# Adapter and conditional linear layer: half of the up projection as rounded products, x turned one sample ahead

## The chip, the core and the metric

One core of a Trainium2 chip. The metric is the device time in microseconds of one execution of the whole program; the median over runs is compared.

## What is computed

32 samples, each of 512 tokens by 512 features, go through two layers with a residual around each. Each sample picks its own weights: `lang` (0 to 8) for an adapter with layer norm, `cat` (0 to 30) for a 512 x 512 linear layer. All inputs and the output are fp32.

```python
def L0(x, lang, W1, b1, W2, b2, gamma, beta):      # H = 512, A = 128
    h = relu(einsum('bsh,bha->bsa', x, W1[lang]) + b1[lang][:, None, :])
    y = x + einsum('bsa,bah->bsh', h, W2[lang]) + b2[lang][:, None, :]
    mean = y.mean(-1, keepdims=True)
    var = ((y - mean) ** 2).mean(-1, keepdims=True)
    return (y - mean) * rsqrt(var + 1e-5) * gamma[lang][:, None, :] + beta[lang][:, None, :]

x = x + L0(x, itok_B_0_8, ...)                     # x: (32, 512, 512)
out = x + (einsum('bti,bio->bto', x, W[cat]) + b[cat][:, None, :])   # cat = itok_B_0_30
```

## The kernel before

The program is written by hand, one instruction list per engine, with semaphores between them; no scheduler moves anything. A sample's tokens are four tiles of 128 (`NT`), its features four chunks of 128 (`NC`). The work is pipelined over three samples. In the step of sample s:

- PE runs, in this order: `linear_tile` 0 and 1 of sample s-2, `up` of s, `turn_norm` 0 and 1 of s-1 (transposes of the normalised activations), `linear_tile` 2 of s-2, `down` of s, `turn_norm` 2 and 3, `linear_tile` 3.
- DVE turns sample s's x into `xT` (`turn_x`, four transposes of 32x32 blocks out of `x_quad`), adds the bias to the four output tiles of s-2 (`output`), forms `x1` and `low_x1` of s-1 chunk by chunk, `low_h`, the sums `y` of s, and at the end of its step the statistics (`variance`, `inverse_deviation`: line 614 is the reciprocal, once per step).
- ScalarE (ACT) rounds the halves of W (`high_w`), normalises s-1's four tiles, does relu (`relu`), rounds `x1` (`high_x1`) and the next sample's w2 (`high_w2_of_next`, line 414), and takes the squares of `y` and the deviation.
- POOL adds the identity to W (the residual, line 348), adds b2 to x (line 358), and forms the low parts of W (line 364) and of w2 (line 338).
- SP issues nearly all transfers: per step two quarters of the next sample's `x_quad` (line 214), w2 (line 227), W (239), x by tokens (219), b2 (231), w1 (223), b (243), `params` (235) and the two output halves (249). In front of them stand three reads of ids (line 210). ScalarE issues the other two quarters of `x_quad` (line 501), right behind its second rounding of W.

Each engine takes its list strictly in order, so an instruction that waits holds up all behind it. The profile calls several tiles by another's name: w1, w2 and W all appear as `w_raw` and `w_hi`, b2 as `b_bc`; size and line tell them apart (w1 is 256 KB, line 223 on SP).

Where one step is joined to the next: `linear_tile(k, 1)` waits for the fourth output of the step before, since it writes that output's bank. SP's `store(k, 2, 1)` waits for the fourth output too, and SP's next step stands behind it. `load_params` waits for the last `low_x1`.

All buffers that are loaded ahead are double (`x_tok`, `w1_raw`, `w2_raw`, `w_raw`, `x_quad`, `xT`, ...). The loops run over two samples per pass, since the buffers alternate; samples 0 and 1 have a prologue written out by hand, in which x is turned on PE, and `keep_clock` puts matmuls of zeros into PE's pauses.

Of the kernel before, what the change touches and what calls it, by code (L numbers as in the profile page):

```python
# [3 lines left out]

class Step:

    def __init__(self, h, p):
        self.h, self.p = h, p  # L10

    def sample(self, back):

        return 2 * self.h + (self.p - back)

    def pairs(self, back):

        return self.h + (self.p - back) // 2

    def count(self, per, back, more):  # L20

        return (2 * per) * self.h + (per * (self.p - back) + more)

    def since(self, k):

        return 2 * self.h + self.p >= k if isinstance(self.h, int) else k <= 2

def adapter_then_conditional_linear(nc, x, lang_ids, cat_ids, W1, b1, W2, b2, gamma, beta, W, b, out):
# [23 lines left out]
    P = 128  # L53
    NT = T // P
    NC = H // P
    NP = 2 * NC + 1
    EPS = 1e-5
    assert A == P and NT == 4 and NC == 4 and S % 2 == 0
# [15 lines left out]
    with ctx:  # L74
# [18 lines left out]
        x_quad = [sb(f"x_quad{i}", [P, NB, NC * SQ]) for i in range(2)]  # L93
        xT = [sb(f"xT{i}", [P, NC, T]) for i in range(2)]
# [43 lines left out]
        def norm_bank(k, c):  # L138

            return n_bank[c % 2]  # L140

        def by_chunk(k):

            return k.since(2) and not (isinstance(k.h, int) and k.h == S // 2)
# [11 lines left out]
        xq_in = [sem(f"xq_in{i}") for i in range(2)]  # L156
# [42 lines left out]
        w_lo_done = sem("w_lo_done")  # L199

# [7 lines left out]
        def _(sp):  # L208
# [3 lines left out]
            def load_x_quads(s, p):  # L212
                for n in (0, 1):
                    sp.dma_start(x_quad[p][quad(n), :, :],
                                 x_quads[bass.ds(s, 1), n].rearrange("o j b f -> j (o b) f")
                                 ).then_inc(xq_in[p], 16)
# [35 lines left out]
            def step(h, p, loads=True, w_load=True, turn=True, linear=True):  # L252

                k, q = Step(h, p), 1 - p
# [19 lines left out]
                if turn:  # L274
# [3 lines left out]
                    load_b(cat_b, q)  # L278
                if linear:
# [18 lines left out]
            load_x(1, 1)  # L298
            sp.wait_ge(cat_in, 16)
            load_w(sample_id(1, 0, G), 0)  # L300
            lang1 = sample_id(0, 1, L)
            load_w1(lang1, 1)
            load_b2(lang1, 1)
# [36 lines left out]

# [535 lines left out]
```

## Time and profile before

| | us |
|---|---|
| median of 3 runs | 631.3 |
| lowest and highest | 631.16 and 632.95 |
| the profiled execution | 632.66 |
| its span, first to last instruction | 630.8 |
| granted TensorE clock, mean | 0.997 |

| engine | busy us | share of the span |
|---|---|---|
| PE | 620.4 | 98% |
| DVE | 524.0 | 83% |
| ACT | 466.2 | 74% |
| POOL | 413.6 | 66% |

A durations column can't be added up for PE: matmuls overlap, so the distance from one start to the next is what one costs. For DVE and ScalarE short overlaps of some 0.07 us between neighbours are usual. Idle time in brackets is that just before the instruction, with what ended it. "Landing" is the time from a transfer's issue until its data is there.

### The profile page before, as it was taken

The page shows a single profiled execution, that of the slowest core. Times are in us where ns is not written, and L with a number is a line of the kernel's source. Part 1 is how long each engine was busy: PE and PEld are TensorE (multiplying, and loading weights), DVE is VectorE, ACT ScalarE, POOL GpSimd, SP SyncE. Part 2 cuts the span into 40 slices and gives each one's busy share as a digit, 9 for nine tenths or more (in the row PEclk, how much of TensorE's full clock was granted, in tenths as well). Part 3 has the DMA queues.
Part 4 walks back from the last instruction along what each step waited for, and adds up shares of the span by engine and source line. Part 5 has one row for each costly group of instructions (what it writes and reads, how often), then busy time and mean ns, then how long its engine had stood idle before and what let it go on. Part 6 is the DMA issues. An engine that isn't in the chain of part 4 may idle for free.

```text
span 630.8 us, 11158 instructions
## 1 busy us (share of the span) xinstructions
PE 620.4 (98%) x2773; PEld 474.5 (75%) x2773; DVE 524.0 (83%) x1155; ACT 466.2 (74%) x709; POOL 413.6 (66%) x326
## 2 busy tenths in 40 slices
PE   8799999999999999999999999999999999999997
PEld 7567877777877777877777877777877777877786
DVE  1879888889888889888889888889888889888873
ACT  3777777787777887777787777787777787777770
POOL 3947766666766666767666866766866766866630
PEclk9899999999999999999999999999999999999999
DMA  8848899888899888899898899988899798899422
GB/s 303 265 143 247 285 295 297 262 255 276 280 294 300 258 255 275 289 287 308 259 252 274 280 291 292 274 263 259 288 286 312 253 257 274 279 289 316 167 85 100
DMA packets 125562, 166.00 MB, mean 263 GB/s; under 512 B 10834, under 2 KB 72284, under 8 KB 121456
## 3 DMA queue, kind: packets, MB, share of 16 engines
q1 hardware_dynamic: 93540, 149.59, 72.6%
q10 hardware_dynamic: 32012, 16.30, 10.7%
q8 instruction: 3, 0.05, 0.0%
q14 instruction: 7, 0.06, 0.0%
HBM read 132.17 MB, written 33.55 MB: 263 GB/s over the span
## 4 chain that ended last, share of the span: by engine, by line
PE 95%; DVE 2%; DMA 1%; issue 1%; ACT 0%; ACTq 0%; SPq 0%; DVEq 0%
PE o_bank L730 18%; PE o_bank L728 18%; PE o_bank L729 18%; PE d_bank L756 17%; PE n_bank L744 9%; PE y_bank L728 2%; PE d_bank L728 2%; PE y_bank L730 2%; PE d_bank L730 2%; PE y_bank L729 2%; PE d_bank L729 2%; DMA x_tok<-in_x 1%; DVE y L587 0%; DVE xT L693 0%; PE n_bank L806 0%
## 5 line engine op out<-in xcount | busy, mean ns | idle before, releaser
L364 POOL TENSOR_TENSOR w_lo<-w_raw,w_hi 128x512 fp32r<-128x512 f32 x128 | 163.1, 1296 | 160.1 <-ACT w_hi L439 160.1
L728 PE MATMUL o_bank<-w_hi,x1T_hi 128*128 128x512 f32 x512 | 205.6, 402 | 0.0
L730 PE MATMUL o_bank<-w_hi,x1T_lo 128*128 128x512 f32 x512 | 200.5, 392 | 0.0
L729 PE MATMUL o_bank<-w_lo,x1T_hi 128*128 128x512 f32 x512 | 199.3, 389 | 0.0
L358 POOL TENSOR_TENSOR x_tok<-x_tok,b_bc 128x512 f32<-128x512 f32 x128 | 163.8, 1303 | 38.0 <-DMA b_bc<-in_L_cond_b 38.0
L429 ACT ACTIVATE norm<-y,neg_mean_rstd,rstd 128x512 f32<-128x512 f32 x127 | 153.4, 1284 | 0.1
L465 ACT ACTIVATE squares<-y,neg_mean 128x512 f32<-128x512 f32 x128 | 91.8, 718 | 76.6 <-DVE neg_mean L593 76.6
L632 DVE SCALAR_TENSOR_TENSOR n_bank<-n_bank,params,xT 128x512 f32<-128x512 f32 x128 | 93.3, 753 | 58.8 <-PE n_bank L744 58.8
L575 DVE STREAM_TRANSPOSE xT<-x_quad 128x512 f32<-128x512 f32 x120 | 125.2, 1087 | 3.2 <-issue 3.1
L756 PE MATMUL d_bank<-xT,w_raw 128*128 128x512 f32 x256 | 115.8, 594 | 3.2 <-DVE xT L693 1.7
L730 PEld LDWEIGHTS o_bank<-w_hi,x1T_lo 128*128 128x128 f32 x512 | 96.1, 188 | 21.2
L729 PEld LDWEIGHTS o_bank<-w_lo,x1T_hi 128*128 128x128 f32 x512 | 96.4, 188 | 18.3
L728 PEld LDWEIGHTS o_bank<-w_hi,x1T_hi 128*128 128x128 f32 x512 | 96.3, 188 | 17.8
L446 ACT ACTIVATE x1T_hi<-n_bank,params 128x512 fp32r<-128x512 f32 x128 | 87.0, 689 | 27.9 <-DVE n_bank L632 26.7
L638 DVE SCALAR_TENSOR_TENSOR x1T_lo<-n_bank,params,x1T_hi 128x512 fp32r<-128x512 f32 x128 | 92.8, 747 | 6.6 <-ACT x1T_hi L446 0.2
L650 DVE TENSOR_TENSOR out_half<-o_bank,b_bc 128x512 f32<-128x512 f32 x128 | 85.9, 671 | 11.1 <-PE o_bank L730 10.9
L756 PEld LDWEIGHTS d_bank<-xT,w_raw 128*128 128x128 f32 x256 | 48.1, 190 | 53.2 <-issue 46.1
L439 ACT ACTIVATE w_hi<-w_raw 128x1024 fp32r<-128x1024 f32 x64 | 67.6, 1056 | 12.9 <-DVE out_half L650 12.7
L744 PEld LDWEIGHTS n_bank<-ident,norm 128*128 128x128 f32 x512 | 60.3, 145 | 20.7 <-issue 15.6
L744 PE MATMUL n_bank<-ident,norm 128*128 128x128 f32 x512 | 66.8, 273 | 0.4 <-ACT norm L429 0.4
L348 POOL TENSOR_TENSOR w_raw<-w_raw,ident 128x512 f32<-128x512 f32 x32 | 50.5, 1577 | 0.0
L587 DVE SCALAR_TENSOR_TENSOR y<-d_bank,x_tok 128x512 f32<-128x512 f32 x64 | 43.7, 683 | 1.9 <-PE d_bank L730 1.9
(59 smaller groups left out, 524.9 us busy)
## 6 DMA issues: line engine op xcount, KB each, us to landing
w_raw<-in_L_cond_W SPq DMA_DIRECT2D x32, 1024.0 KB, 6.6
out<-out_half SPq DMA_DIRECT2D x63, 512.0 KB, 3.9
x_tok<-in_x SPq DMA_DIRECT2D x31, 1024.0 KB, 8.9
w_raw<-in_L_cond_W SPq DMA_DIRECT2D x64, 256.0 KB, 6.4
b_bc<-in_L_cond_b SPq DMA_DIRECT2D x64, 256.0 KB, 9.5
x_quad<-in_x SPq DMA_DIRECT2D x60, 256.0 KB, 3.9
x_quad<-in_x ACTq DMA_DIRECT2D x60, 256.0 KB, 3.9
x_tok<-in_x ACTq DMA_DIRECT2D x1, 512.0 KB, 3.3
```

The lines of the kernel that those rows point to most:

```text
L358: pool.tensor_tensor(x_tok[p][:, t, :], x_tok[p][:, t, :], b2_bc[p][:, :], ALU.add).then_inc(x_b2_done, 1)
L364: pool.tensor_tensor(w_lo[q][:, c, :], w_raw[q][:, c, :], w_hi[q][:, c, :].bitcast(F32), ALU.subtract).then_inc(w_lo_done, 1)
L429: act.activation(dst, src, ACT.Identity, scale=rstd[:, t:t + 1], bias=neg_mean_rstd[:, t:t + 1]).then_inc(norm_done, 1)
L465: act.activation(squares[:, t, :], y[:, t, :], ACT.Square, bias=neg_mean[:, t:t + 1], accum_out=sq_sum[:, t:t + 1]).then_inc(sq_done, 1)
L575: dve.transpose(xT[p][:, c, :].rearrange("p (b j) -> p b j", j=SQ), x_quad[p][:, :, c::NC]).then_inc(xT_done, 1)
L632: dve.scalar_tensor_tensor(norm_bank(k, c)[:, :], norm_bank(k, c)[:, :], params[q][:, c:c + 1], xT[q][:, c, :], ALU.mult, ALU.add).then_in ...
L638: dve.scalar_tensor_tensor(x1T_lo[q][:, c, :], norm_bank(k, c)[:, :], params[q][:, NC + c:NC + c + 1], x1T_hi[q][:, c, :].bitcast(F32), AL ...
L728: pe.matmul(acc, lhs_hi, rhs_hi, start=first, stop=False)
L729: pe.matmul(acc, lhs_hi, rhs_lo, start=False, stop=False)
L730: return pe.matmul(acc, lhs_lo, rhs_hi, start=False, stop=last)
L744: ins = pe.transpose(norm_bank(k, c)[:, t * P:(t + 1) * P], norm[:, t, c * P:(c + 1) * P] if by_chunk(k) else norm[:, t, c::NC], ident[:, :])
L756: ins = pe.matmul(d_bank[0][:, :], w1_raw[k.p][:, c, :], xT[k.p][:, c, :], start=c == 0, stop=c == NC - 1)
```

## The change

1. Of `up`'s four chunks, 0 and 1 (`NS = 2`) become products of rounded parts; chunks 2 and 3 stay plain fp32 and go first. The parts are made one sample ahead: ScalarE rounds chunks 0 and 1 of the next sample's w1 (128x256) and of its turned x (128x1024), POOL subtracts to get the low parts.
2. So the next sample's x must be turned a step earlier: DVE's `turn_next_x` in step s turns sample s+1. `xT` has three tiles in place of two, `x_quad` one in place of two. Its reload waits until the four turns of the step are done; it stands behind b in SP's list and behind relu in ScalarE's.
3. The buffers now alternate by two and by three, so all loops take six samples per pass (`ROUND = 6`); steps 2 to 7 are written out and, on all engines but PE, the last six too; four passes are left for the loop on PE and three on the others.
4. POOL's order: the low parts of W are made in two pairs with b2's additions between; behind w2's low part come w1's and x's.
5. The prologue is rebuilt: x's first turns by token tile and not by chunk, `w1` and `b2` of sample 1 loaded ahead of the first W, x of sample 1 turned half before and half after `down` of 0, quarters of sample 2 loaded and turned there, four normalisations all on ScalarE, 8 and 12 zero matmuls in place of 4 and 6.

In SP's list, one regular step; the rows begin behind the three reads of ids. `w_raw ... 128x512` is w2 at line 227 (245 after) and w1 at line 223 (241 after), `128x2048` is W. Before:

```order
L214 ISA [waits xT_done]
L214 DMA x_quad<-in_x 32x16x128
L214 ISA
L214 DMA x_quad<-in_x 32x16x128
L227 ISA [waits y_done]
L227 DMA w_raw<-in_L_cond_W 128x512
L239 ISA [waits w_lo_done]
L239 DMA w_raw<-in_L_cond_W 128x2048
L219 DMA x_tok<-in_x 128x4x512
L231 ISA
L231 DMA b_bc<-in_L_cond_b 128x512
L223 DMA w_raw<-in_L_cond_W 128x512
```

After, SP's list at the same place:

```order
L245 ISA [waits y_done]
L245 DMA w_raw<-in_L_cond_W 128x512
L257 ISA [waits w_lo_done]
L257 DMA w_raw<-in_L_cond_W 128x2048
L237 DMA x_tok<-in_x 128x4x512
L249 ISA
L249 DMA b_bc<-in_L_cond_b 128x512
L241 DMA w_raw<-in_L_cond_W 128x512
L261 ISA [waits out_done]
L261 DMA b_bc<-in_L_cond_b 128x512
L232 DMA x_quad<-in_x 32x16x128 [waits xT_done]
L232 DMA x_quad<-in_x 32x16x128
```

The two quarters of `x_quad` moved from the head to behind b; the other loads keep their order, w1 as the fourth behind w2.

ScalarE's list in a regular step, from behind its second rounding of W. `w_hi ... 128x512` is the rounding of the next w2. Before:

```order
L501 DMA x_quad<-in_x 32x16x128 [waits xT_done]
L501 DMA x_quad<-in_x 32x16x128
L456 ACTIVATE d_bank<-d_bank,params 128x512 [waits params_in0,up_done]
L459 ACTIVATE hT_hi<-d_bank 128x512 [waits relu_done]
L446 ACTIVATE x1T_hi<-n_bank,params 128x512 [waits x1_done,params_in1]
L446 ACTIVATE x1T_hi<-n_bank,params 128x512 [waits x1_done]
L414 ACTIVATE w_hi<-w_raw 128x512 [waits down_done,w2_in1]
L465 ACTIVATE squares,sq_sum<-y,neg_mean 128x512 [waits mean_done,y_done] x3
L446 ACTIVATE x1T_hi<-n_bank,params 128x512 [waits x1_done] x2
```

After, ScalarE's list at the same place; `w_hi ... 128x256` is the rounding of the next w1's two chunks:

```order
L501 ACTIVATE d_bank<-d_bank,params 128x512 [waits params_in1,up_done]
L504 ACTIVATE hT_hi<-d_bank 128x512 [waits relu_done]
L558 DMA x_quad<-in_x 32x16x128 [waits xT_done]
L558 DMA x_quad<-in_x 32x16x128
L491 ACTIVATE x1T_hi<-n_bank,params 128x512 [waits x1_done,params_in0]
L491 ACTIVATE x1T_hi<-n_bank,params 128x512 [waits x1_done]
L459 ACTIVATE w_hi<-w_raw 128x512 [waits down_done,w2_in0]
L521 ACTIVATE w_hi<-w_raw 128x256 [waits w1_in0]
L526 ACTIVATE xs_hi<-xT 128x1024 [waits xT_done]
L510 ACTIVATE squares,sq_sum<-y,neg_mean 128x512 [waits mean_done,y_done] x3
L491 ACTIVATE x1T_hi<-n_bank,params 128x512 [waits x1_done] x2
```

The two transfers moved behind relu, and two roundings with a wait for w1 and one for xT stand in front of the first square.

The diff, cut to its core:

```diff
     def __init__(self, h, p):
         self.h, self.p = h, p
+        self.b, self.x = p % 2, p % 3
...
-        x_quad = [sb(f"x_quad{i}", [P, NB, NC * SQ]) for i in range(2)]
-        xT = [sb(f"xT{i}", [P, NC, T]) for i in range(2)]
+        x_quad = sb("x_quad", [P, NB, NC * SQ])
+        xT = [sb(f"xT{i}", [P, NC, T]) for i in range(3)]
+
+        xs_hi = sb("xs_hi", [P, NS, T], F32R)
+        xs_lo = sb("xs_lo", [P, NS, T], F32R)
+        w1_hi = sb("w1_hi", [P, NS, A], F32R)
+        w1_lo = sb("w1_lo", [P, NS, A], F32R)
...
                     cat_b = sample_id(1, k.sample(1), G)
                 if loads:
-                    sp.wait_ge(xT_done, k.count(NC, 0, 0))
-                    load_x_quads(k.sample(-1), q)
...
+                    sp.wait_ge(xT_done, k.count(NC, 0, 2 * NC))
+                    load_x_quads(k.sample(-2))
                 if linear:
                     store(k, 2, 0)
...
             step(0, 1, linear=False)
-            with sp.Fori(1, S // 2 - 1) as h:
-                step(h, 0)
-                step(h, 1)
-            step(S // 2 - 1, 0)
-            step(S // 2 - 1, 1, loads=False)
-            step(S // 2, 0, loads=False, w_load=False)
-
-            last = Step(S // 2, 1)
+            for p in range(2, 2 + ROUND):
+                step(0, p)
+            with sp.Fori(1, S // ROUND - 1) as h:
+                for p in range(2, 2 + ROUND):
+                    step(h, p)
+            for p in range(2, 2 + ROUND):
+                s = S - ROUND + p - 2
+                step(S // ROUND - 1, p, quads=s + 2 < S, loads=s + 1 < S)
+            step(S // ROUND, 2, quads=False, loads=False, w_load=False)
...
+            def low_w1(k):
+
+                pool.wait_ge(w1_hi_done, k.count(1, 0, 0))
+                pool.tensor_tensor(w1_lo[:, :, :], w1_raw[1 - k.b][:, 0:NS, :], w1_hi[:, :, :].bitcast(F32),
+                                   ALU.subtract).then_inc(w1_lo_done, 1)
+
+            def low_xs(k):
+
+                pool.wait_ge(xs_hi_done, k.count(1, 0, 0))
+                for c in range(NS):
+                    pool.tensor_tensor(xs_lo[:, c, :], xT[(k.x + 1) % 3][:, c, :], xs_hi[:, c, :].bitcast(F32),
+                                       ALU.subtract).then_inc(xs_lo_done, 1)
...
-                        for c in range(NC):
-                            low_w(c)
+                        low_w(0)
+                        low_w(1)
                     if adapter:
                         plus_b2(2)
                         plus_b2(3)
+                    if turn:
+                        low_w(2)
+                        low_w(3)
                 if follow:
                     low_w2(q, k.count(1, -1, 1))
+                    if k.since(1):
+                        low_w1(k)
+                        low_xs(k)
...
+            def high_w1_of_next(k):
+
+                act.wait_ge(w1_in[1 - k.b], 16 * k.pairs(-1) + 16)
+                act.activation(w1_hi[:, :, :], w1_raw[1 - k.b][:, 0:NS, :], ACT.Copy).then_inc(w1_hi_done, 1)
+
+            def high_xs_of_next(k):
+
+                act.wait_ge(xT_done, k.count(NC, 0, NC + NS))
+                act.activation(xs_hi[:, :, :], xT[(k.x + 1) % 3][:, 0:NS, :], ACT.Copy).then_inc(xs_hi_done, 1)
 
...
                     normalise(k, t)
                 high_w(k, 2)
-                if follow:
-                    load_next_x_quads(k)
                 if adapter:
                     relu(k)
+                if follow and not k.last(S - 2):
+                    load_next_x_quads(k)
...
                 high_x1(k, 1)
                 if follow:
                     high_w2_of_next(k)
+                    high_w1_of_next(k)
+                    high_xs_of_next(k)
                 if adapter:
...
-                load_x_quads(k.sample(-1), 1 - k.p)
+                act.wait_ge(xT_done, k.count(NC, 0, 2 * NC))
+                load_x_quads(k.sample(-2))
 
...
-                act.activation(xT[0][:, c, :], first_xT_bank(c)[:, :], ACT.Copy).then_inc(xT_done, 1)
+                copy_first_xT(0, c)
             high_w2(0, 0)
             relu(k0)
+            load_x_quads(2)
+            copy_first_xT(1, 0)
+            copy_first_xT(1, 1)
+            high_w(k1, 0)
+            high_w2_of_next(k0)
             for t in range(NT):
                 square(k0, t)
             deviation(k0)
-            high_w(k1, 0)
-            high_w2_of_next(k0)
-
-            normalise(k1, 0)
-            normalise(k1, 1)
-            normalise(k1, 2)
-            load_next_x_quads(k1)
             relu(k1)
+            for t in range(NT):
+                normalise(k1, t)
             high_w(k1, 2)
+            square(k1, 0)
+            square(k1, 1)
             high_x1(k1, 0)
             high_x1(k1, 1)
-            high_w2_of_next(k1)
-            square(k1, 0)
-            square(k1, 1)
+            square(k1, 2)
+            square(k1, 3)
             high_x1(k1, 2)
             high_x1(k1, 3)
-            square(k1, 2)
-            square(k1, 3)
             deviation(k1)
-
-            with act.Fori(1, S // 2 - 1) as h:
-                step(h, 0)
-                step(h, 1)
-            step(S // 2 - 1, 0)
-            step(S // 2 - 1, 1, follow=False)
-            step(S // 2, 0, adapter=False, follow=False)
+            high_w2_of_next(k1)
+            load_next_x_quads(k1)
+            high_w1_of_next(k1)
+            high_xs_of_next(k1)
+
+            for p in range(2, 2 + ROUND):
+                step(0, p)
+            with act.Fori(1, S // ROUND - 1) as h:
+                for p in range(2, 2 + ROUND):
+                    step(h, p)
+            for p in range(2, 2 + ROUND):
+                step(S // ROUND - 1, p, follow=S - ROUND + p - 1 < S)
+            step(S // ROUND, 2, adapter=False, follow=False)
...
 
-            def turn_x(k, c):
-
-                p = k.p % 2
+            def turn_next_x(k, c):
+
                 if c == 0:
-                    dve.wait_ge(xq_in[p], 16 * NQ * k.pairs(0))
-                dve.transpose(xT[p][:, c, :].rearrange("p (b j) -> p b j", j=SQ),
-                              x_quad[p][:, :, c::NC]).then_inc(xT_done, 1)
+                    dve.wait_ge(xq_in, k.count(16 * NQ, 0, 0))
+                dve.transpose(xT[(k.x + 1) % 3][:, c, :].rearrange("p (b j) -> p b j", j=SQ),
+                              x_quad[:, :, c::NC]).then_inc(xT_done, 1)
 
...
-                                  ALU.mult, ALU.add).then_inc(norm_done, 1)
+            low_h(k1)
+            turn_next_x(k1, 0)
+            y_pair(k1, 0)
+            y_pair(k1, 1)
             x1(k1, 0)
             x1(k1, 1)
-            low_h(k1)
             low_x1(k1, 0)
             low_x1(k1, 1)
-            y_pair(k1, 0)
             x1(k1, 2)
             x1(k1, 3)
             low_x1(k1, 2)
             low_x1(k1, 3)
-            y_pair(k1, 1)
+            turn_next_x(k1, 1)
             variance(k1)
             inverse_deviation(k1)
-
-            with dve.Fori(1, S // 2) as h:
-                step(h, 0)
-                step(h, 1)
-            step(S // 2, 0, adapter=False)
+            turn_next_x(k1, 2)
+            turn_next_x(k1, 3)
+
+            for p in range(2, 2 + ROUND):
+                step(0, p)
+            with dve.Fori(1, S // ROUND - 1) as h:
+                for p in range(2, 2 + ROUND):
...
             def up(k):
 
-                pe.wait_ge(w1_in[k.p], 16 * k.pairs(0) + 16)
+                acc, parts = d_bank[0][:, :], NS if k.since(2) else 0
+                pe.wait_ge(w1_in[k.b], 16 * k.pairs(0) + 16)
                 if k.since(1):
                     pe.wait_ge(y_done, k.count(NT, 0, 0))
-                for c in range(NC):
+                for c in range(parts, NC):
                     pe.wait_ge(xT_done, k.count(NC, 0, c + 1))
-                    ins = pe.matmul(d_bank[0][:, :], w1_raw[k.p][:, c, :], xT[k.p][:, c, :],
-                                    start=c == 0, stop=c == NC - 1)
+                    ins = pe.matmul(acc, w1_raw[k.b][:, c, :], xT[k.x][:, c, :], start=c == parts, stop=c == NC - 1 and not parts)
+                if parts:
+                    pe.wait_ge(w1_lo_done, k.count(1, 2, 1))
+                for c in range(parts):
+                    pe.wait_ge(xs_lo_done, k.count(NS, 2, c + 1))
+                    ins = split_product(acc, w1_hi[:, c, :], w1_lo[:, c, :], xs_hi[:, c, :], xs_lo[:, c, :],
+                                        False, c == parts - 1)
                 ins.then_inc(up_done, 1)
 
...
-                step(h, 1)
-
-
-            k = Step(S // 2, 0)
+            for c in range(NC):
+                turn_norm(k1, c)
+            keep_clock(12, o_bank[1])
+
+            for p in range(2, 2 + ROUND):
+                step(0, p)
+            with pe.Fori(1, S // ROUND) as h:
+                for p in range(2, 2 + ROUND):
+                    step(h, p)
+
+
+            k = Step(S // ROUND, 2)
             linear_tile(k, 0)
             linear_tile(k, 1)
```

## Rows read from the trace of the kernel before

**Rows 1.** The page's busy shares, and its chain by engine:

```profile
PE 620.4 (98%) x2773; PEld 474.5 (75%) x2773; DVE 524.0 (83%) x1155; ACT 466.2 (74%) x709; POOL 413.6 (66%) x326
...
PE 95%; DVE 2%; DMA 1%; issue 1%; ACT 0%; ACTq 0%; SPq 0%; DVEq 0%
```

**Rows 2.** The timeline of PE around `up` (start, us, instructions):

```profile
306.34 0.40 PE L730 MATMUL o_bank<-w_hi,x1T_lo 128*128 128x512 f32 x1
306.57 3.60 PE L756 MATMUL d_bank<-xT,w_raw 128*128 128x512 f32 x8
310.01 1.04 PE L744 MATMUL n_bank<-ident,norm 128*128 128x128 f32 x8
```

**Rows 3.** The timeline of DVE, each step's reciprocal:

```profile
302.49 0.17 DVE L614 RECIPROCAL r<-std 128x4 f32<-128x4 f32 x1
...
321.52 0.17 DVE L614 RECIPROCAL r<-std 128x4 f32<-128x4 f32 x1
...
340.30 0.17 DVE L614 RECIPROCAL r<-std 128x4 f32<-128x4 f32 x1
```

**Rows 4.** ScalarE's x_quad loads in the prologue: duration, start, landing:

```profile
L501 ACTq DMA_DIRECT2D x_quad<-in_x x2: 339/886/1432, 22.2 to 22.5; - x2
...
DMA to landing us min/median/max: 9.4/10.1/10.7
```

**Rows 5.** The timeline of ScalarE in a regular step:

```profile
308.38 1.06 ACT L439 ACTIVATE w_hi<-w_raw 128x1024 fp32r<-128x1024 f32 x1
...
313.59 0.62 ACT L414 ACTIVATE w_hi<-w_raw 128x512 fp32r<-128x512 f32 x1
316.46 0.73 ACT L465 ACTIVATE squares<-y,neg_mean 128x512 f32<-128x512 f32 x1 [2.24 <-DVE neg_mean L593]
```

**Rows 6.** The timeline of SP's loads in the same step:

```profile
306.36 0.89 SPq L214 DMA_DIRECT2D x_quad<-in_x  x2
307.43 0.36 SPq L227 DMA_DIRECT2D w_raw<-in_L_cond_W  x1
...
309.05 0.36 SPq L231 DMA_DIRECT2D b_bc<-in_L_cond_b  x1
309.51 0.47 SPq L223 DMA_DIRECT2D w_raw<-in_L_cond_W  x1
```

**Rows 7.** SP's line 223 (w1) in that step, issue to landing:

```profile
DMA to landing us min/median/max: 9.8/9.8/9.8
```

**Rows 8.** The timeline of POOL in that step:

```profile
315.77 1.58 POOL L348 TENSOR_TENSOR w_raw<-w_raw,ident 128x512 f32<-128x512 f32 x1
318.81 2.56 POOL L358 TENSOR_TENSOR x_tok<-x_tok,b_bc 128x512 f32<-128x512 f32 x2 [1.45 <-DMA b_bc<-in_L_cond_b]
```

**Rows 9.** SP's line 231 (b2) in that step, issue to landing:

```profile
DMA to landing us min/median/max: 9.6/9.6/9.6
```

**Rows 10.** The timeline of SP in the prologue, w2 and w1:

```profile
18.72 0.37 SPq L227 DMA_DIRECT2D w_raw<-in_L_cond_W  x1
...
20.77 0.59 SPq L223 DMA_DIRECT2D w_raw<-in_L_cond_W  x1
```

**Rows 11.** SP's line 223 (w1) in the prologue, issue to landing:

```profile
DMA to landing us min/median/max: 11.1/11.1/11.1
```

**Rows 12.** The page's DMA queue of ScalarE: packets, MB, share:

```profile
q10 hardware_dynamic: 32012, 16.30, 10.7%
```

**Rows 13.** The timeline of DVE, the fourth output of a step:

```profile
320.80 0.68 DVE L650 TENSOR_TENSOR out_half<-o_bank,b_bc 128x512 f32<-128x512 f32 x1
```

**Rows 14.** The timeline of DVE, two of a step's four turns:

```profile
322.40 2.07 DVE L575 STREAM_TRANSPOSE xT<-x_quad 128x512 f32<-128x512 f32 x2
```

**Rows 15.** The page's DMA issues, ScalarE's x_quad loads:

```profile
x_quad<-in_x ACTq DMA_DIRECT2D x60, 256.0 KB, 3.9
```

**Rows 16.** The timeline of PE in the prologue, behind a pause:

```profile
27.36 0.50 PE L728 MATMUL d_bank<-w_hi,hT_hi 128*128 128x512 f32 x1 [1.69 <-DVE hT_lo L580]
```

**Rows 17.** Busy times, clock (PEclk) and DMA by stretch, 28 to 29 us:

```profile
28.00:29.00 1.00, 1.00 (x4) 0.81 (x3) 0.97 (x2) 0.17 (x1) 1.00 (x1) 0.50 1.08 350
```

More of the change, by code:

```diff
@@ L10, in __init__, with last @@
         self.h, self.p = h, p
+        self.b, self.x = p % 2, p % 3
     def sample(self, back):
-        return 2 * self.h + (self.p - back)
+        return ROUND * self.h + (self.p - back)
     def pairs(self, back):
-        return self.h + (self.p - back) // 2
+        return ROUND // 2 * self.h + (self.p - back) // 2
     def count(self, per, back, more):
-        return (2 * per) * self.h + (per * (self.p - back) + more)
+        return (ROUND * per) * self.h + (per * (self.p - back) + more)
     def since(self, k):
-        return 2 * self.h + self.p >= k if isinstance(self.h, int) else k <= 2
+        return ROUND * self.h + self.p >= k if isinstance(self.h, int) else k <= 2
+    def last(self, s):
+        return isinstance(self.h, int) and ROUND * self.h + self.p == s
 def adapter_then_conditional_linear(nc, x, lang_ids, cat_ids, W1, b1, W2, b2, gamma, beta, W, b, out):
@@ L56, in adapter_then_conditional_linear @@
     NP = 2 * NC + 1
+    NS = 2
     EPS = 1e-5
[L58 removed]
+    assert A == P and NT == 4 and NC == 4 and S % ROUND == 2 and S > 2 * ROUND
     NQ, SQ = 4, 32
@@ L138, in norm_bank @@
         def norm_bank(k, c):
-            return n_bank[c % 2]
+            return y_bank[c - 2] if c >= 2 and not k.since(2) else n_bank[c % 2]
         def by_chunk(k):
-            return k.since(2) and not (isinstance(k.h, int) and k.h == S // 2)
+            return k.since(2) and not k.last(S)
         def down_bank(t):
@@ L155, in adapter_then_conditional_linear @@
         first_b1_in = sem("first_b1_in")
-        xq_in = [sem(f"xq_in{i}") for i in range(2)]
+        xq_in = sem("xq_in")
         x_in = [sem(f"x_in{i}") for i in range(2)]
@@ L250, in store, with step @@
                              ).then_inc(stored[half], 16)
-            def step(h, p, loads=True, w_load=True, turn=True, linear=True):
-                k, q = Step(h, p), 1 - p
+            def step(h, p, quads=True, loads=True, w_load=True, turn=True, linear=True):
+                k = Step(h, p)
+                p, q = k.b, 1 - k.b
                 if loads:
@@ L586, in y_tile @@
                 dve.wait_ge(x_b2_done, k.count(NT, 0, t + 1))
-                dve.scalar_tensor_tensor(y[:, t, :], down_bank(t)[:, :], 1.0, x_tok[k.p][:, t, :],
+                if k.since(1) and not k.since(2):
+                    dve.wait_ge(norm_done, t + 1)
+                dve.scalar_tensor_tensor(y[:, t, :], down_bank(t)[:, :], 1.0, x_tok[k.b][:, t, :],
                                          ALU.mult, ALU.add, accum_out=y_sum[:, t:t + 1]
@@ L596, in y_pair @@
             def y_pair(k, i):
-                if i == 0 and k.since(1):
+                if i == 0 and k.since(2):
                     dve.wait_ge(norm_done, k.count(NT, 0, 0))
@@ L690, in _ @@
             y_pair(k0, 1)
-            for c in range(NC):
+            dve.wait_ge(xT_done, NC + 2)
+            for c in (2, 3):
                 dve.wait_ge(first_xT_turned, NC + c + 1)
@@ L710, in _ @@
             low_x1(k1, 3)
-            y_pair(k1, 1)
+            turn_next_x(k1, 1)
             variance(k1)
             inverse_deviation(k1)
-            with dve.Fori(1, S // 2) as h:
-                step(h, 0)
-                step(h, 1)
-            step(S // 2, 0, adapter=False)
+            turn_next_x(k1, 2)
[3 more added lines that the diff above has]
+            with dve.Fori(1, S // ROUND - 1) as h:
+                for p in range(2, 2 + ROUND):
+                    step(h, p)
+            for p in range(2, 2 + ROUND):
+                step(S // ROUND - 1, p, follow=S - ROUND + p - 1 < S)
+            step(S // ROUND, 2, adapter=False, follow=False)
             for t in range(NT):
-                output(Step(S // 2, 1), t)
+                output(Step(S // ROUND, 3), t)
         @block.tensor
@@ L811, in _ @@
             pe.wait_ge(ident_done, 3)
-            for c in range(NC):
-                turn_first_x(k0, c)
+            turn_first_x()
             up(k0)
```

142 lines of the change are left out of this document (76 added, 66 removed).

## Prediction

> **What bounds the kernel now.** I read the page's busy shares and its chain first: PE is busy 98% of the span and holds 95% of the chain that ended last [rows 1]. Then one regular step of PE in order of time [rows 2]: each rounded matmul starts 0.23 us after the one before, the eight pieces of `up` stand from 306.57 to 310.01, and nothing waits. The third view is the distance from one step's reciprocal to the next [rows 3]: 340.30 - 302.49 = 37.81 us for two steps, 18.9 us for one; the two differ by 0.26 us (19.03 and 18.78), once per pass of the loop of two. So PE's own work is the bound, and a shorter `up` is worth its full length if no other cycle is longer than the new step. The profiled execution took 632.66 us, of which the span is 630.8; the median of the runs is 631.3, 1.4 us less. I add to 632.66 and take off 1.4 at the end.
>
> **The change, part by part.**
>
> *Two chunks of `up`.* A plain fp32 chunk is two pieces: 3.44 / 4 = 0.86 us. A product of rounded parts is three matmuls of 0.23 us, 0.68 us [rows 2]. Two chunks save 2 x 0.18 = 0.36 us in each of 30 steps, 10.7 us, all on PE's path.
>
> *The loop of six.* Of 15 loop passes 4 stay. If the 0.26 us belongs to the loop head, that gives back up to 11 x 0.26 = 2.9 us; at worst nothing.
>
> *x turned one sample ahead.* DVE's four transposes stay four per step, at the same place; what they read was loaded a whole step earlier, from one quarter tile. SP and ScalarE reload it once the step's turns are through, about 7.5 us into the step, and it is needed some 15 us later. Where such loads ran against a full queue they took 9.4 to 10.7 us [rows 4], so this costs nothing in a regular step.
>
> *ScalarE gets two more operations*, between the rounding of w2 and the first square. From 128x512 in 0.62 us and 128x1024 in 1.06 us [rows 5], rounding w1's 128x256 is about 0.40 us and x's 128x1024 1.0 us of issue distance: 1.4 us. Their cover is the 2.24 us that the first square waits for DVE [rows 5]; 0.8 us of that is left. Alone, this is free.
>
> *POOL gets three more subtractions*, 0.7 + 2 x 1.3 = 3.3 us per step, in front of the identity's addition. It is busy 66% of the span [rows 1], so some 6 us a step are idle, and the reordering fills an idle stretch in front of w_lo. From the end of ScalarE's rounding of w2, 314.2, it takes a handoff of some 0.3 us, w2's 1.3, the 3.3 and the addition's 1.58 [rows 8]: 320.7, ahead of ScalarE's next rounding of W, which comes behind the fourth output, at about 321.5. Free, barely.
>
> *The new wait, which decides.* The rounding of w1 waits until w1 **of the next sample** has landed, and this load is not moved: it stands fifth in SP's list of the same step. Until now nobody needed it before the next `up`, 15 us later. In the trace it is issued at 309.51 [rows 6] and lands 9.8 us later [rows 7], at 319.3. ScalarE reaches the place of the new operation at 313.59 + 0.62 = 314.2 [rows 5], and with 0.8 us of cover would have to have the data by 315.0. Neighbouring evidence that landings are real: POOL waits 1.45 us until 318.81 for b2 [rows 8], the transfer just ahead of w1 in that queue, issued at 309.05 and landed 9.6 us after [rows 6, 9].
>
> The change takes SP's x_quad loads from in front of these transfers (SP starts 1.07 us earlier, 306.36 for 307.43 [rows 6]). But ScalarE's two x_quad loads go from behind the normalisation's dispatch to behind relu, into the middle of these transfers. So I must ask how long w2, W, x, b2 and w1 take from an empty queue with ScalarE's loads arriving some us later. The trace holds exactly that case once, in the prologue: w2 is issued at 18.72, w1 at 20.77 [rows 10], w1 lands 11.1 us after [rows 11], at 31.9, and ScalarE's quarters start at 22.2 beside it [rows 4]. That is 13.15 us from the first issue. The regular step, with SP's quarters ahead instead, gives nearly the same: 319.3 - 306.36 = 12.95 us. In the new kernel ScalarE's quarters start about 4.5 us after w2 and not 3.4, so I estimate that 0.25 us less of them comes in front: **12.9 us**.
>
> From the other side: a step's ScalarE quarters are worth 10.7% of the span [rows 12] over 30 steps, 2.25 us. If none of them delayed w1, it would take 13.15 - 2.25 = 10.9 us.
>
> Who waits behind it: squares 0 to 2, x1T_hi 2 and 3, square 3 and the deviation are queued behind that operation on ScalarE. x1T_lo 2 and 3 on DVE wait for x1T_hi, the fourth output (ends 320.80 + 0.68 = 321.48 [rows 13], 0.04 us before the reciprocal at 321.52, and so at 302.45 in the step before [rows 3]) is queued behind them, SP's second store waits for that output, and SP's next loads stand behind the store. That closes a cycle, step to step:
> - fourth output ended, to SP's first load: 306.36 - 302.45 = 3.9 us [rows 3, 6]; in the steps of the other half of the loop some 3.5; I take 3.7 us
> - first load issued to w1 landed: 12.9 us
> - landing to ScalarE's start, as POOL's after b2: 318.81 - (309.05 + 9.6), 0.15 us
> - rounding w1 and x: 0.40 + 1.0 us
> - first square's start to the end of the fourth output: 321.48 - 316.46 = 5.0 us, which was back to back on ScalarE up to x1T_hi and on DVE from there [rows 5, 13].
>
> Sum: 3.7 + 12.9 + 0.15 + 1.4 + 5.0 = **23.15 us a step**, 4.25 us over 18.9. PE's 18.6 us no longer matter; PE will stand idle about 4.6 us a step before its second tile, since that tile's bank waits for the fourth output.
>
> Steps 3 to 30 do this, 28 of them: 28 x 4.25 = 119 us. In step 2 SP has one thing more in front: the quarters for sample 3 wait for the four turns at the prologue's end, the last two of them (2.07 us [rows 14]) after the statistics. 2.07 + 0.9 (two issues) + 0.5 (params) + 3.0 (three id reads) instead of the 0.4 us of before gives some 6.1 us, then 12.9 + 6.55: a step of about 26 to 27 us for 18.2 before, 9 us more. The rest of the rebuilt prologue is copies and turns in another order; PE's waits there are under 2 us each and I give it -1 us, with 3 us to either side. Steps 31 and on have no rounding ahead: 0.
>
> Total: 632.66 + 119 + 9 - 1 = 759.7; on the median's footing **758 us**.
>
> **What the skill adds.** Rows show ScalarE's quarters, alone in a regular step, landing after 3.9 us at the median [rows 15] and beside a full SP queue after 9.4 to 10.7 [rows 4]: they share. The Trainium skill (DMA: Bandwidth & Descriptors, Queues, rings and completion order) says that each DMA engine takes packets in turn from the queues that have work. By that rule the small packets are nearly all through before w1 is, and the sum stays; if SP's queue instead went first, it would be the 10.9 us. The trace agrees with the rule, by the same landings.
>
> **The rivals.**
> - *The wait, but w1 lands sooner* (10.9 us): a step of 21.15 us, 2.25 x 28 = 63 us less, 695 us. For it: nobody has measured the new order, and PE's pause may push relu and the quarters later. Against it: the prologue's 13.15.
> - *No wait that counts; faster*. The mechanism: the five transfers, 2.9 MB, land by 315.0, 8.6 us after SP's first issue. Then PE stays the bound: 632.66 - 10.7 - 2.9 - 1 - 1.4 = 617 us. It decides at 8.6 us; the shortest row is 12.95. Also a misreading of which sample's w1 is waited for would end here.
> - *A small wait*: 9 to 10.5 us and a step of 19.3 to 20.8; 640 to 690 us.
> - *The clock falls too, slower still*. After PE stood 1.69 us [rows 16], the granted clock was 0.50, the 1.2 GHz level, in the next whole microsecond [rows 17]. With 4.6 us idle per step I expect such a stretch in every step. From the fourth output on PE has four tiles of twelve matmuls, one `up` and two groups of turns ahead, 4 x 2.74 + 3.08 + 1.6 = 15.6 us, due by 22.5, so up to 6.7 us of its work at half speed are hidden. If 10 us of it ran at half speed, the step would be 0.2 + 25.6 + 0.7 = 26.5 us and the time 28 x 3.35 = 94 us longer, near 850 us.
>
> **How the numbers follow.** The forecast (730 to 790 us, with the cycle's terms at 3.5 to 3.9, 12.0 to 13.7 and the prologue's 3 us): 0.72. Sooner landing (690 to 730): 0.13. Small wait (640 to 690): 0.05. PE-bound and faster: 0.04. Same: 0.01. Clock or another wait on top, over 790 us: 0.05. The range takes the first two, 690 to 790 us, about 0.85. Within 0.3% is what a measurement here can't tell from no change. Faster 0.04, same 0.01, slower 0.95.
>
> **What the profile would show.** Right: ScalarE's waits led by `w_hi` or `squares` on the w1 load, some 4 us in each of about 29 steps, beginning with the 128x256 operation; PE idle 4 to 5 us before `o_bank`'s second tile; reciprocals 23 us apart; w1 landing 11 us after its issue; PE's eight pieces of `up` gone to four plus six rounded ones, about 3.1 us; chain shared by ScalarE, DVE, SP and DMA. Wrong: reciprocals 18.6 apart with PE at 98% (the load landed in time); PE waiting for POOL's xs_lo (POOL the bound); or a granted clock of 0.5 through most of a step.

## The result: 11% slower, each step waits for w1

| | before | after |
|---|---|---|
| median, same chip | 632.05 us | 701.48 us |
| lowest and highest | 631.16 to 632.95 | 699.54 to 702.79 |
| span of the profiled execution | 630.8 us | 700.9 us |
| granted TensorE clock, mean | 0.997 | 0.97 |

The ratio is 1.1103 (1.1084 to 1.1123; such brackets are 95% intervals). The kernel before takes about 631.2 or 632.9 us from one execution to the next (granted clock 1.0 or 0.997), and with a fourth run beside the first three its median is 632.05. The page of the kernel after, its busy shares and its chain by engine, against [rows 1]:

```profile
PE 635.4 (91%) x2853; PEld 496.4 (71%) x2853; DVE 522.2 (75%) x1152; ACT 498.3 (71%) x772; POOL 509.0 (73%) x416
...
DMA 32%; SPq 16%; ACT 15%; PE 13%; DVE 10%; issue 10%; POOL 2%; ACTq 1%; DVEq 0%; POOLq 0%
```

PE held 95% of the chain before and holds 13% now; a third of it is a transfer. Who waited for whom in the kernel after (total, times, longest):

```profile
ACT w_hi L521 <- DMA w_raw<-in_L_cond_W: 109.7, 28, 6.5
POOL w_lo L368 <- ACT w_hi L521: 89.2, 29, 5.6
DVE x1T_lo L704 <- ACT x1T_hi L491: 82.1, 30, 5.4
...
PE o_bank L798 <- DVE x1T_lo L704: 50.9, 24, 4.0
```

L521 is the rounding of w1, and its releaser (what ended the wait) is the load. The three rows under it are the same lateness passed on, from ScalarE to POOL, to DVE and to PE.

One step of the kernel after: first SP's loads of w2 (L245) and w1 (L241), then the time from w1's issue to its landing in that step, then ScalarE's timeline against [rows 5]:

```profile
327.19 0.38 SPq L245 DMA_DIRECT2D w_raw<-in_L_cond_W  x1
...
329.25 0.80 SPq L241 DMA_DIRECT2D w_raw<-in_L_cond_W  x1
```

```profile
DMA to landing us min/median/max: 11.0/11.0/11.0
```

```profile
333.90 0.62 ACT L459 ACTIVATE w_hi<-w_raw 128x512 fp32r<-128x512 f32 x1
340.24 0.42 ACT L521 ACTIVATE w_hi<-w_raw 128x256 fp32r<-128x256 f32 x1 [5.72 <-DMA w_raw<-in_L_cond_W]
340.56 1.04 ACT L526 ACTIVATE xs_hi<-xT 128x1024 fp32r<-128x1024 f32 x1
341.51 0.70 ACT L510 ACTIVATE squares<-y,neg_mean 128x512 f32<-128x512 f32 x1
...
343.63 1.24 ACT L491 ACTIVATE x1T_hi<-n_bank,params 128x512 fp32r<-128x512 f32 x2
```

w1 is issued at 329.25 and ScalarE starts at 340.24, the moment it lands. The squares now stand back to back behind it; the first had waited for DVE in [rows 5]. DVE at the end of the same step, and the reciprocal that opened it, against [rows 3, 13]:

```profile
323.78 0.17 DVE L680 RECIPROCAL r<-std 128x4 f32<-128x4 f32 x1
...
344.33 1.41 DVE L704 SCALAR_TENSOR_TENSOR x1T_lo<-n_bank,params,x1T_hi 128x512 fp32r<-128x512 f32 x2 [4.70 <-ACT x1T_hi L491]
345.65 0.68 DVE L716 TENSOR_TENSOR out_half<-o_bank,b_bc 128x512 f32<-128x512 f32 x1
...
346.38 0.17 DVE L680 RECIPROCAL r<-std 128x4 f32<-128x4 f32 x1
```

This step takes 22.6 us, one of the longer ones. On average steps 3 to 30 take 21.18 us (reciprocals at 64.20 and 657.13, 28 steps) for 18.90.

PE's pause in that step, and the clock behind it:

```profile
341.08 0.39 PE L800 MATMUL o_bank<-w_hi,x1T_lo 128*128 128x512 f32 x1
345.22 0.76 PE L798 MATMUL o_bank<-w_hi,x1T_hi 128*128 128x512 f32 x1 [3.76 <-DVE x1T_lo L704]
```

```profile
345.00:347.00 2.00, 1.78 (x4) 1.49 (x5) 1.90 (x9) 1.50 (x4) 2.00 (x3) 0.50 0.00 0
```

PE was busy until 341.5 and then idle for 3.8 us; in the next two microseconds the granted clock (the third number from the end) was 0.50, the 1.2 GHz level. It costs nothing here: from ScalarE's rounding to the next reciprocal are 6.14 to 6.15 us in each of the 28 regular steps, with such a stretch or without.

What was to be gained is there too. `up` in the kernel after, against [rows 2]:

```profile
305.34 1.88 PE L829 MATMUL d_bank<-xT,w_raw 128*128 128x512 f32 x4
...
308.44 1.04 PE L816 MATMUL n_bank<-ident,norm 128*128 128x128 f32 x8
```

From its start to the turns behind it are 3.10 us for 3.44.

The 70.1 us of span by place, from the reciprocals of both kernels:

| | before | after | difference |
|---|---|---|---|
| to the reciprocal of step 1 | 38.65 | 36.32 | -2.3 |
| step 2 | 18.18 | 27.88 | +9.7 |
| steps 3 to 30 | 529.3 | 592.9 | +63.6 |
| step 31 | 18.86 | 17.87 | -1.0 |
| behind it | 25.8 | 25.9 | +0.1 |

### The profile page after: what moved, and what is told of

Its sections match the earlier page's. It is cut to its first block, busy times and chain, and to the rows that moved or that the text cites. A ratio compares the mean times of both kernels' runs of the same rounds, so it can differ in the third digit from the quotient of the medians.

```text
span 700.9 us, 10824 instructions
## 1 busy us (share of the span) xinstructions
PE 635.4 (91%) x2853; PEld 496.4 (71%) x2853; DVE 522.2 (75%) x1152; ACT 498.3 (71%) x772; POOL 509.0 (73%) x416
## 4 chain that ended last, share of the span: by engine, by line
DMA 32%; SPq 16%; ACT 15%; PE 13%; DVE 10%; issue 10%; POOL 2%; ACTq 1%; DVEq 0%; POOLq 0%
DMA w_raw<-in_L_cond_W 32%; ACT squares L510 9%; DVE x1T_lo L704 6%; SPq L228 6%; PE o_bank L798 3%; ACT x1T_hi L491 3%; PE o_bank L799 3%; PE o_bank L800 3%; DVE y L653 2%; ACT norm L474 2%; SPq L253 2%; SPq L267 2%; SPq L257 2%; SPq L249 1%; PE d_bank L829 1%
## 5 line engine op out<-in xcount | busy, mean ns | idle before, releaser
L798 PE MATMUL o_bank<-w_hi,x1T_hi 128*128 128x512 f32 x512 | 214.2, 418 | 50.9 <-DVE x1T_lo L704 50.9
L800 PE MATMUL o_bank<-w_hi,x1T_lo 128*128 128x512 f32 x512 | 205.7, 402 | 0.0
L799 PE MATMUL o_bank<-w_lo,x1T_hi 128*128 128x512 f32 x512 | 205.6, 402 | 0.0
L402 POOL TENSOR_TENSOR w_lo<-w_raw,w_hi 128x512 fp32r<-128x512 f32 x128 | 163.1, 1299 | 16.2 <-ACT w_hi L484 15.2
L800 PEld LDWEIGHTS o_bank<-w_hi,x1T_lo 128*128 128x128 f32 x512 | 99.7, 195 | 22.9
L799 PEld LDWEIGHTS o_bank<-w_lo,x1T_hi 128*128 128x128 f32 x512 | 100.1, 195 | 17.7
L491 ACT ACTIVATE x1T_hi<-n_bank,params 128x512 fp32r<-128x512 f32 x126 | 82.3, 680 | 26.4 <-DVE n_bank L698 13.4
L521 ACT ACTIVATE w_hi<-w_raw 128x256 fp32r<-128x256 f32 x30 | 12.5, 417 | 114.7 <-DMA w_raw<-in_L_cond_W 109.7
L368 POOL TENSOR_TENSOR w_lo<-w_raw,w_hi 128x256 fp32r<-128x256 f32 x30 | 22.3, 742 | 89.2 <-ACT w_hi L521 89.2
L375 POOL TENSOR_TENSOR xs_lo<-xT,xs_hi 128x512 fp32r<-128x512 f32 x60 | 75.8, 1285 | 6.0 <-ACT xs_hi L526 6.0
L362 POOL TENSOR_TENSOR w_lo<-w_raw,w_hi 128x512 fp32r<-128x512 f32 x31 | 40.2, 1296 | 50.8 <-ACT w_hi L459 50.8
```

The lines of the kernel that those rows point to most:

```text
L402: pool.tensor_tensor(w_lo[q][:, c, :], w_raw[q][:, c, :], w_hi[q][:, c, :].bitcast(F32), ALU.subtract).then_inc(w_lo_done, 1)
L491: act.activation(x1T_hi[q][:, c, :], norm_bank(k, c)[:, :], ACT.Identity, bias=params[q][:, NC + c:NC + c + 1]).then_inc(x1_hi_done, 1)
L798: pe.matmul(acc, lhs_hi, rhs_hi, start=first, stop=False)
L799: pe.matmul(acc, lhs_hi, rhs_lo, start=False, stop=False)
L800: return pe.matmul(acc, lhs_lo, rhs_hi, start=False, stop=last)
```

## Experiments

The theory on record is a cycle: fourth output, SP's next loads, w1's landing, ScalarE's rounding, squares, x1T_hi, x1T_lo, fourth output. Its terms, measured in each run from the timelines as means over steps 3 to 30 (from the reciprocal to SP's issue of w2; from there to w1's landing; from the landing to ScalarE's operation; from there to the next reciprocal):

| run | to w2's issue | to landing | to ScalarE | to the reciprocal | step |
|---|---|---|---|---|---|
| the changed kernel | 3.33 | 11.68 | 0.02 | 6.14 | 21.18 |
| w1_before_b2 | 3.35 | 9.94 | 0.02 | 6.14 | 19.45 |
| act_quads_late | 3.33 | 11.09 | 0.02 | 6.24 | 20.68 |
| before_wait | 4.72 | 11.73 | 0.02 | 5.19 | 21.66 |
| w1_second | 3.32 | 3.60 | 4.36 | 7.36 | 18.64 |
| before_wait_w1_second | 4.72 | 5.09 | 1.71 | 7.38 | 18.90 |

In the first four the third column is nil: the load is what ScalarE waits for, in every step. In the last two the data lies ready, 4.36 and 1.71 us ahead of ScalarE. The ratios below are to the kernel before, run on the same chip: 631.68 us beside w1_second, w1_before_b2, act_quads_late and before_wait, 631.24 us beside the others.

### w1_second

```diff
                     load_w2(lang, q)
+                    load_w1(lang, q)
                 if w_load:
...
                     load_b2(lang, q)
-                    load_w1(lang, q)
```

> The changed kernel with one edit: SP issues w1 of the next sample second, right behind w2, and not fifth. Theory (the cycle over the fourth output, SP's loads, w1's landing and ScalarE's rounding sets the step at 3.3 us + landing + 6.2 us): w1 lands some 4 to 5 us after SP's first issue instead of 11.7, so ScalarE's wait goes, the cycle falls to about 14 us and PE's own 18.6 us a step is the bound again: 28 x (21.2 - 18.6) = 72 us and about 8 us of step 2 less, 620 us. Rival (the loop of six, the rebuilt prologue, or POOL's and ScalarE's extra work is what costs): within 5 us of 701 us, since nothing of those is touched.

Measured: 634.06 us, ratio 1.003 (1.001 to 1.0051). The regular steps did what was expected, 18.64 us for 18.6; the wait is gone from ScalarE's timeline:

```profile
319.20 0.62 ACT L459 ACTIVATE w_hi<-w_raw 128x512 fp32r<-128x512 f32 x1
319.72 0.40 ACT L521 ACTIVATE w_hi<-w_raw 128x256 fp32r<-128x256 f32 x1
```

The rival falls: one line moved in SP's list takes 67 us off. But the time is 14 us over the 620 expected. Step 2 is some 9 us of that: it took 28.84 us, 1 us more than in the kernel after, and I had expected 8 us less, as if it waited for w1. The rest is small: 1.7 us in the regular steps, 0.7 us each in the prologue and in step 31, and the profiled execution of the kernel after was 1.3 us over its median. The chain of step 2, from the trace of w1_second, in order of time:

```profile
37.97 1.98 DVE xT L639 x2
39.98 0.37 ACTq L558
40.37 0.55 ACTq L558
40.97 0.43 ACT w_hi L521
41.46 0.73 POOL w_lo L368
42.41 2.49 POOL xs_lo L375 x2
44.90 1.54 POOL w_raw L386
...
47.48 4.90 ACT norm L474 x4
52.42 1.97 PE n_bank L816 x8
```

ScalarE's loads for sample 3 wait until the last two turns of sample 2 are done, and stand ahead of the roundings of w1 and x in its list. POOL adds the identity to W (L386) only behind their low parts, ScalarE rounds W only behind the identity, and the normalisation only behind that. PE's turns begin at 52.4.

### w1_before_b2

```diff
                     load_x(k.sample(-1), q)
-                    load_b2(lang, q)
                     load_w1(lang, q)
+                    load_b2(lang, q)
```

> The changed kernel, w1 issued ahead of b2 (fourth and not fifth). A dose of the same: b2's transfer was worth 1.3 to 1.9 us between landings. Theory: the step gets shorter by just what w1's landing does, about 1.5 us, to 19.7 us, and the time falls to about 660 us. Rival (order of loads doesn't matter): 701 us.

Measured: 656.07 us, ratio 1.0373 (1.0342 to 1.0404). The landing came 1.74 us sooner and the step got 1.73 us shorter. One microsecond of w1's landing is one microsecond of the step.

### act_quads_late

```diff
                     relu(k)
-                if follow and not k.last(S - 2):
-                    load_next_x_quads(k)
...
                     high_xs_of_next(k)
+                if follow and not k.last(S - 2):
+                    load_next_x_quads(k)
```

> The changed kernel, ScalarE's two x_quad loads issued behind the rounding of x instead of behind relu, so that they don't run beside w2, W, x, b2 and w1. If the two queues share the engines packet by packet and the quarters are worth 2.25 us, most of them in front of w1: landing 9.9 us after the first issue for 11.7, a step of 19.4 us, 650 us. If they cost w1 nothing: landing 11.7 us, 701 us. In either case the turns of the next step may wait for the quarters, which are issued later, by less than 1 us.

Measured: 690.66 us, ratio 1.0934 (1.0913 to 1.0954); it fits neither. With ScalarE's quarters wholly out of the way (issued 11.3 us after w2, behind w1's landing) w1 landed 11.09 us after w2's issue for 11.68, so they had cost 0.6 us and not the 1.8 I expected. They do share: beside SP's loads they landed 9.9 us after their issue at the median in the kernel after, 3.9 in [rows 15]. They took little from w1 by it, since over half of them came behind it: in the kernel after, over the 27 regular steps that load quarters, 42% of these packets were through on average when w1 landed, and the second quarter landed 3.9 us after w1.

### before_wait

The kernel before with this alone; the copy goes to a tile that nobody reads.

```diff
                 if follow:
                     high_w2_of_next(k)
+                    act.wait_ge(w1_in[1 - k.p], 16 * k.pairs(-1) + 16)
+                    act.activation(w1_seen[:, :, :], w1_raw[1 - k.p][:, 0:2, :], ACT.Copy)
```

> The kernel before, with only the wait added: at the place where the change rounds w1, ScalarE waits for the next sample's w1 and copies two of its chunks into a tile that nobody reads. Loop of two, old prologue, plain up. Theory: w1 lands 16.4 us after a step's reciprocal (SP's first load 3.7 us, x_quad's issues 1.0 us, 11.7 us to the landing), then 0.3 us for the copy and 4.9 us to the next reciprocal: 21.6 us a step for 18.9, about 708 us. Rival (something else in the change costs): 631 us, at most 1 us more, since 0.4 us of copy lie under a wait of 2.2 us.

Measured: 708.81 us, ratio 1.1204 (1.1155 to 1.1252), a step of 21.66 us. The four executions lie between 705.62 and 711.98, and the profiled one is the longest. The wait put into the old kernel is as dear as the whole change. The wait list names it first but one:

```profile
POOL w_lo L365 <- ACT w_hi L440: 239.8, 63, 7.1
ACT w_seen L490 <- DMA w_raw<-in_L_cond_W: 147.9, 29, 6.6
```

The POOL row above it is larger, but not on the cycle, whose four terms add up to the whole step without it; POOL waited there in the kernel before too, 160.1 us in 63 times.

### before_wait_w1_second

before_wait with the edit of w1_second.

> The kernel before with the added wait and copy as in before_wait (there 708.8 us), and w1 issued second, behind w2. If the wait costs only because the load behind it is late, w1 now lands about 4.6 us after SP's first load of weights, before ScalarE comes to the place, and the time is that of the kernel before, 632 us, within 2 us. If the wait itself or the copy costs, it stays well above.

Measured: 631.09 us for 631.24, ratio 0.9998 (0.9985 to 1.0011). The wait and the copy together cost nothing once the load is early: w1 lands 1.7 us before ScalarE comes to it.

### plain_up

```diff
-                acc, parts = d_bank[0][:, :], NS if k.since(2) else 0
+                acc, parts = d_bank[0][:, :], 0
...
-                    high_w1_of_next(k)
-                    high_xs_of_next(k)
...
-                    if k.since(1):
-                        low_w1(k)
-                        low_xs(k)
```

> The kernel of w1_second without the rounded parts: up is four plain fp32 chunks, ScalarE and POOL make no parts of w1 and x; x turned ahead, loop of six and the rebuilt prologue stay. This is the worth of the rounding. In w1_second PE's own step is 18.58 us, in the kernel before 18.90 us; so the regular steps cost 28 x 0.32 = 9 us more. Step 2 is 28.8 us in w1_second, since POOL's identity stands behind the parts of x there; without them about 5 us of it go. Sum: 634 + 9 - 5 = 638 us. If the rounding gave nothing, 629 us.

The kernel that ran differs from this text in one point: it was cut from the changed kernel, so w1 is still issued fifth. Nothing waits for it before the next `up` in this kernel, and the time expected doesn't hang on it.

Measured: 638.64 us, ratio 1.0107 (1.0086 to 1.0127). From one `up` to the next are 18.91 us on PE in every regular step, as in the kernel before, though this kernel has the loop of six. In w1_second they are 18.59 us where nothing is late. So the rounding is worth 0.32 us a step and the loop of six nothing. The rest of the change, prologue and turned x, is a loss of its own: step 2, `up` to `up`, is 25.4 us for 20.0, and the rebuilt prologue gives back 1.8 us of that. The profiled execution, 636.29 us, is the shortest of the four; where the others lost 2.2 to 2.6 us more no trace shows.

### early_turns

w1_second, and in short:

```diff
             load_w(sample_id(1, 0, G), 0)
             load_w2(lang1, 1)
+            load_x_quads(2)
             sp.wait_ge(table_done, 1)
...
+            for c in range(NC):
+                turn_next_x(k1, c)
             variance(k0)
             inverse_deviation(k0)
             low_h(k1)
-            turn_next_x(k1, 0)
...
                     if turn:
                         plus_identity()
                     if adapter:
+                        low_w1(Step(h, k.p - 1))
+                        low_xs(Step(h, k.p - 1))
                         plus_b2(0)
```

ScalarE's quarters of sample 2 also go ahead of its first copies, and the parts at the end of POOL's step go out.

> w1_second with the way into step 2 freed: the quarters of sample 2 are issued ahead of the table's loads, DVE turns them in its pause before the first statistics, so that the quarters of sample 3 and SP's loads of step 2 don't wait behind them; POOL makes w1's and x's low parts at the start of the next step, behind the identity, and not in front of it. Step 2 took 28.8 us for 18.2 in the kernel before and PE stood 5.7 us there before the turns of the normalised tiles. Theory (step 2 is long because SP, ScalarE and POOL stand behind the last two turns): 7 to 10 us less, 625 us, 1% faster than the kernel before. Rival (step 2 is long for its transfers): within 3 us of 634 us.

Measured: 626.16 us, ratio 0.990 (0.9881 to 0.9919). Step 2 fell from 28.84 to 20.66 us, while the prologue before it grew from 37.0 to 39.0: 6 us in the sum; the regular steps give 1.8 us more, and the time is 8 us shorter. The rival had 634 us within 3 us, and falls. Several things were moved together here, and what each of them gave isn't shown. Of POOL's and ScalarE's parts alone plain_up tells something: without them step 2 is 24.6 us from reciprocal to reciprocal for 28.84, so about 4 of the 8 us can come from their place.

### three_parts

early_turns, and in short:

```diff
-    NS = 2
+    NS = 3
...
-        param_rows = sb("param_rows", [L, 2 * H + A])
+        param_rows = squares[0:L, :, :].rearrange("p t h -> p (t h)")[:, 0:2 * H + A]
```

> early_turns with three of up's four chunks as products of rounded parts (the prologue's table rows moved into the tile of squares to make room). PE saves another 0.16 us in each of 28 steps, 4.5 us; ScalarE gets 0.6 us more, POOL 1.6 us more, about 17.6 us a step on POOL for PE's 18.4. If PE stays the bound: 621 us. If POOL or ScalarE takes over: 625 us or more, with PE waiting for xs_lo or for the normalised tiles.

Measured: 620.34 us, ratio 0.9819 (0.9793 to 0.9844). This beats both kernels, by 1.8% the one before. PE's step is 18.42 us on average (18.59 in early_turns). The page's busy shares, and how long PE waited for POOL's parts:

```profile
PE 609.4 (99%) x2883; PEld 493.9 (80%) x2883; DVE 520.3 (84%) x1152; ACT 518.9 (84%) x772; POOL 552.9 (89%) x446
```

```profile
PE d_bank L795 <- POOL xs_lo L375: 1.0, 3, 0.5
```

POOL is at 89% and only just in time. In a regular step it is busy 17.7 us, against 16.2 in early_turns. A fourth part would by the same dose make some 19.2 us (an estimate), more than PE's step; it was not tried.

## Why the prediction held, and which terms were off

758 us was forecast, in a range of 690 to 790; 701.5 was measured. The mechanism is the one forecast, and before_wait and w1_second show it from both sides. The size is not: 701.5 lies outside the 730 to 790 us of the forecast itself (chance 0.72) and inside the bracket of its first rival (0.13), which the range took in. The slowdown forecast, 127 us, was nearly twice the one measured, 69 us. By the prediction's own steps:

- **Two chunks of `up`:** 0.36 us forecast, 0.32 measured, `up` to `up` on PE.
- **The loop of six:** up to 2.9 us were allowed; nothing. The 0.26 us between odd and even steps in [rows 3] is in DVE's reciprocals alone. PE's `up` came every 18.91 us, so the difference never was on PE's path. I had read a loop head of PE out of DVE's rows.
- **ScalarE's and POOL's extra work:** hidden, as said; w1_second runs at PE's pace with all of it.
- **The new wait:** right in its place, its releaser and what is queued behind. Its size failed in one term above all: w2's issue to w1's landing, 12.9 us forecast and 11.68 measured, 1.2 of the 2.0 us by which the step was too long. The row I sized it by [rows 10, 11] was called an empty queue and was not one. There SP had issued two quarters of x at 16.2 us, 2.5 us ahead of w2, and they landed 3.4 to 4.0 us after. It was also a single step, and single steps of the kernel after lie between 10.5 and 15.0 us. What of the 13.15 us was due to which isn't shown. The better row was at hand: in the regular step w1 landed 319.3 - 307.43 = 11.9 us after w2's issue [rows 6, 7]. The 12.95 us that I compared with it began at the issue of SP's quarters. And ScalarE's quarters, which I had let weigh nearly their full 2.25 us, weigh 0.6 (act_quads_late). That their packets are nearly all through before w1 was wrong: 42% were, worth 0.8 us. The lower bound of 10.9 us for a way without them came near the 11.09 measured by luck, since it is 13.15 less 2.25 and neither holds.
- **The small terms:** SP's first load came 3.33 us after the reciprocal, 3.4 after the fourth output, not 3.7. Landing to ScalarE is 0.02 us, not 0.15. From the rounding to the next reciprocal are 6.14 us, not 6.45: the two roundings take 1.27 us, not 1.4, and the stretch from the first square to the end of the fourth output 4.82, not 5.0, since the squares no longer wait for DVE in between. Together 0.8 us.
- 28 steps x 1.97 us = 55 us, which is the whole miss but 2 us.
- **Step 2:** 9 us more forecast, 9.7 measured. But I named w1's wait for it, and it is SP's, ScalarE's and POOL's wait for the turns of sample 2: in w1_second, where w1 is early, step 2 is 28.84 us still. The link was wrong, and the size right by luck: the prediction's own terms, 6.1 + 12.9 + 6.55, make 25.6 us and not 26 to 27, which is 7.4 us more than before. It misled the expectation of w1_second by 9 us.
- **Prologue and end:** -1 us forecast for the prologue, -2.3 measured; nothing for step 31, -1.0 measured.
- **PE's pause:** 4.6 us a step forecast in front of the second tile. It was 50.9 us in 24 waits, 2.1 us each. It lies within the first, in front of its third chunk, which reads x1T_lo of the sample just formed. DVE makes x1T_lo ahead of the fourth output, so this wait comes first.
- **The clock:** a stretch at 0.50 was expected in every step. There were nine in the 28 regular steps, each at a pause of PE of 2.0 to 4.0 us; at other pauses, up to 3.05 us long, the granted clock did not fall. All nine were hidden, as the rival's bound of 6.7 us said.

Of the rivals the first, w1 landing sooner at a step of 21.15 us, met the measured step of 21.18. Its time was added up wrongly: the step is 2.0 us shorter than the forecast's and not 2.25, so 28 of them give 56 us less, 702 us and not 695; measured are 701.5. This match is luck too. Its reason was that ScalarE's quarters delay w1 by nothing; they delay it by 0.6 us, so that its 10.9 us is 0.8 too short, and its other terms, the forecast's own, are 0.8 too long.

## What to carry to other kernels

When work is moved to a sample ahead, look up when each of its inputs lands, not only when it is issued: a load that nobody needed for 15 us was fifth in a list, and a rounding of 0.4 us that waited for it set the step of the whole kernel. A wait put in by itself and the load moved by itself are two one-line experiments that settle such a case. And an interval read on one engine is not the interval of another: the loop of two had no price on PE.

## What the runs showed beyond this

SP's issue of a transfer is not always short. In w1_second, with SP's loads otherwise in the order of the changed kernel, two issues of the quarters and one store took this long:

```profile
315.68 3.33 SPq L232 DMA_DIRECT2D x_quad<-in_x  x2
319.21 3.44 SPq L267 DMA_DIRECT2D out<-out_half  x1
```

In the kernel before a quarter's issue took 0.35 us at the median and 0.49 at most. In the kernel after it took up to 1.8, and in w1_second up to 3.7, at places where 3 MB were issued just ahead. DVE then waited for the quarters, 1.4 us in each of 18 regular steps of w1_second; PE waited 0.6 us in all of its regular steps together. What limits the issue there was not tried.

From w2's issue to w1's landing took 10.5 to 13.0 us in the regular steps of the kernel after, with one of 15.0, and the late steps were shorter than the early ones. ScalarE's quarters are not needed for such a spread: in act_quads_late, where none is under way, it is 10.3 to 13.0 us. No run tells what makes it.
